# Tridiagonalisation in one program: the panel loop as a hardware loop, and written out

## The reference

```python
deg = jnp.sum(A, axis=0) + jnp.sum(A, axis=1) - jnp.diagonal(A)
L_norm = d_inv_sqrt[:, None] * (jnp.diag(deg) - A) * d_inv_sqrt[None, :]
_, U = jnp.linalg.eigh(L_norm)            # 1024 x 1024, symmetric
agg = jnp.einsum('mn,bnd->bmd', U.T, features)
...
return jnp.einsum('nm,bmd->bnd', U, out)
```

## Time and profile before

| | |
|---|---|
| median of 3 runs | 9222.39 us (9209.03 to 9224.98) |
| profiled execution: its own time | 9224.03 us |
| its span, first to last instruction | 9222.3 us |
| its mean granted clock of PE | 0.756 of full speed |
| first L401 to last L401 (panel 0 to panel 31) | 838.4 to 5724.6 us |
| busy over the span | PE 5701.9, DVE 6703.0, ACT 2708.2, POOL 1214.8 us |

### The profile page before, as it was taken

The page is one execution under the profiler, slowest core; times in us unless marked ns, Lnnn a source line. Parts: engine busy times, 40 slices in busy tenths (PEclk is TensorE's granted clock), DMA queues, the critical chain, the costliest instruction groups (busy, mean ns, idle before and its releaser), DMA issues. The chain is left out here.

```text
span 9222.3 us, 334698 instructions
## 1 busy us (share of the span) xinstructions
PE 5701.9 (62%) x138962; PEld 3872.5 (42%) x138962; DVE 6703.0 (73%) x32749; ACT 2708.2 (29%) x7811; POOL 1214.8 (13%) x5408
## 2 busy tenths in 40 slices
PE   5696778777788877777776554344434330036956
PEld 2364555555566666655665544101000000033446
DVE  3566666677677777777778888888888889954055
ACT  1442111111111111111113334566666650010046
POOL 0000111111122222222223333100000000000000
PEclk8898999999999999888665555555555555578989
DMA  1000000000000000000000000000000000000000
GB/s 38 1 1 20 4 4 4 4 4 4 4 4 4 4 4 4 4 4 4 4 4 4 4 4 4 1 0 0 0 0 0 0 0 0 0 0 1 0 19 19
DMA packets 24662, 42.83 MB, mean 5 GB/s; under 512 B 2464, under 2 KB 20128, under 8 KB 23200
## 3 DMA queue, kind: packets, MB, share of 16 engines
q1 hardware_dynamic: 23200, 21.70, 0.7%
HBM read 17.50 MB, written 4.19 MB: 2 GB/s over the span
## 5 line engine op out<-in xcount | busy, mean ns | idle before, releaser
L313 PE MATMUL tri_y<-L 128*32 128x256 f32 (+7 forms) x36792 | 1976.5, 345 | 11.8 <-issue 10.9
L313 PEld LDWEIGHTS tri_y<-L 128*32 128x32 f32 x36792 | 1195.6, 122 | 226.5 <-issue 50.6
L405 ACT ACTIVATE tri_mu<-tri_ring,tri_tiny 128x1 f32<-128x1 f32 x1022 | 267.1, 261 | 1985.4 <-PE tri_ring L296 1985.4
L1536 PE MATMUL ev_pairs<-ev_sgn,ident 128*128 128x448 bf16 x1024 | 428.8, 574 | 579.7 <-ACT ev_sgn L1501 579.7
L1660 DVE SCALAR_TENSOR_TENSOR ev_seq<-ev_seq,ev_rowG,ev_u 128x112 f32<-128x112 f32 x2048 | 682.8, 333 | 91.0 <-DVE ev_u L1645 2.3
L408 ACT ACTIVATE tri_sM<-tri_half_M,tri_s 128x8 f32<-128x8 f32 (+5 forms) x767 | 229.0, 299 | 1464.7 <-DVE tri_s L601 1464.7
L1645 DVE TENSOR_TENSOR ev_u<-ev_shifted,ev_seq 128x112 f32<-128x112 f32 x2048 | 560.4, 274 | 86.6 <-DVE ev_seq L1667 14.0
L1490 ACT ACTIVATE ev_shifted<-ev_x,ev_rowG 128x112 f32<-128x112 f32 x2112 | 613.0, 372 | 31.4 <-DVE ev_rowG L1617 31.4
L296 PE MATMUL tri_ring<-L 128*32 128x32 f32 (+25 forms) x35704 | 599.6, 206 | 3.3 <-issue 3.1
L296 PE MATMUL tri_k<-tri_kp,tri_half 128*32 128x1 f32 x6136 | 191.1, 184 | 615.3 <-DVE tri_x L609 614.8
L296 PEld LDWEIGHTS tri_ring<-L 128*32 128x32 f32 x35704 | 516.0, 118 | 3.7 <-issue 3.7
(11 more groups left out here) (660 smaller groups left out, 14148.8 us busy)
## 6 DMA issues: line engine op xcount, KB each, us to landing
adj<-in_adj_dram SPq DMA_DIRECT2D x12, 1024.0 KB, 8.1
x<-in_x_dram SPq DMA_DIRECT2D x8, 512.0 KB, 7.2
out_dram<-x SPq DMA_DIRECT2D x8, 512.0 KB, 6.6
gcn_w<-in_L_gnn_W_dram SPq DMA_DIRECT2D x2, 128.0 KB, 2.2
spec_w<-in_L_gnn_W_dram SPq DMA_DIRECT2D x2, 64.0 KB, 1.8
dot_wt<-in_L_gnn_W_dram SPq DMA_DIRECT2D x1, 64.0 KB, 1.8
dot_rows<-in_L_gnn_b_lin_dram SPq DMA_DIRECT2D x1, 64.0 KB, 2.7
dot_rows<-in_L_gnn_b_dram SPq DMA_DIRECT2D x1, 64.0 KB, 3.4
```

What stands on the lines that cost most here:

```text
L313: last = nc.tensor.matmul(y[32 * g:32 * g + 32, 0:T * 32], A[:, b + t, XC:XC + 1].broadcast_to([P, 32]), cols, start=(t == 0), stop=(t == ...
L405: nc.scalar.activation(mu[:, :], sigma, ACT.Sqrt, bias=tiny[:, :]).then_inc(root_ready, 1)
L1536: last = nc.tensor.matmul(sums[h], S["ident16"][:, :], sgn[:, h * (GRP // 2) + k:(h + 1) * (GRP // 2) + k, :].rearrange("p s w -> p (s w)" ...
```

## The change

The loop over a body's panels becomes a Python loop: each of the 32 panels is its own body, with a count of 1, so each has its own code on each of the four engines, and all counts are constants. The order of the work within a panel is what it was. One line fewer above shifts all later lines by one.

```diff
-        bodies = [(0, 0, 1, 1, NB_P), (0, 1, LP - 1, 0, NB_P)] + [(b, 0, LP, 0, NB_P) for b in range(1, NT - 1)] \
-            + [(NT - 1, 0, LP - 1, 0, NB_P), (NT - 1, LP - 1, 1, 0, NB_P - 1)]
+        bodies = [(b, p, 1, 1 if b == p == 0 else 0, NB_P - 1 if (b, p) == (NT - 1, LP - 1) else NB_P) for b in range(NT) for p in range(LP)]
...
             for k, (b, it0, cnt, s0, s1) in enumerate(bodies):
                 T = NT - b
-                with pe.Fori(0, cnt) as it:
+                for it in range(cnt):
                     pn = it + panels_before[k]
```

More of the change, by code:

```diff
@@ L257, in _ @@
                 T = NT - b
-                with pool.Fori(0, cnt) as it:
+                for it in range(cnt):
                     pool.wait_ge(window_ready, it + (panels_before[k] + 1))
@@ L390, in _ @@
                 T = NT - b
-                with act.Fori(0, cnt) as it:
+                for it in range(cnt):
                     pn = it + panels_before[k]
@@ L456, in _ @@
                 act_t = slice(b, NT)
-                with dve.Fori(0, cnt) as it:
+                for it in range(cnt):
                     pn = it + panels_before[k]
```

## The result

| | before | after |
|---|---|---|
| median of the runs | 9215.71 us (4 runs, 9206.53 to 9224.98) | 9134.27 us (4 runs, 9132.60 to 9150.17) |
| profiled execution | 9224.03 us | 9133.02 us |
| span | 9222.3 us | 9131.3 us |
| first to last start of L401 (L400 after) | 4886.3 us | 4789.1 us |

The changed kernel takes 0.9915 of the time before, 95% interval 0.9898 to 0.9933. Between the two profiled executions it is 91.0 us; the stage of the panels alone gives 97 us of it, and the rest of the program was 6 us longer in this execution. That rest is the same code in every kernel here, and it took 4336 to 4347 us in the twelve profiles (4336.0 and 4345.1 in the two of the kernel before), so it moves by some 10 us by itself.

The account below looks back on a forecast made before the run. A chain of short steps across engines bounds the panels, with late fetches after jumps back. 47.7 + 5.7 - 1.7 = 51.7 us off the profiled 9224.0 us gives 9172.3, median 9171 us; range 9154 to 9196 us.

Parts of the forecast that it names:

- What bounds the kernel, and what a jump is: Panels are a chain of short steps with no engine full; a jump back makes the instruction fetch start late.
- PE's branch of 3.3 to 4.5 us as the price: At panel ends, a jump back costs PE some 3.3 to 4.5 us; falling through takes 76 ns.
- The 22 jumps back go: 47.7 us: At panel entries, later panels become like the first of their width, gaining 47.7 us over 20 jumps.
- T = 8: 0: Jumped-to T = 8 panels were 3.7 us shorter, put down to the clock and counted as 0.
- ACT's registers: 5.7 us: Between last update and L397, constants replace ACT's window registers: 30 entries at 0.19 us, 5.7 us gained.
- DVE's wait on its own, 1.7 us lost: In 19 tails, the wait ahead of DVE's copy becomes its own instruction: 1.7 us lost, bounds 0 to 3.6.
- The code grows, at nothing: ACT and POOL fetch every panel's code, 22 panels more; costed at nothing.
- Rival A: At panel starts the stall stays, only the instructions themselves are saved: 9216 us; 6 in 100.
- Rival B: Straight code starves as ACT and POOL fetch 60 blocks: 86 us slower, 9308 us; 4 in 100.
- Rival C: In T=5 and T=4 the clock takes back 23.2 us (9194), or T=5 gains 12.7 us (9158); 10 in 100 each side.

Follow-up runs that it names:

- experiment 4: ACT's and POOL's loops alone written out, against the kernel before, PE and DVE keeping loops: 9210.26 us, ratio 0.9994.
- experiment 1: Kernel before with loops kept, plus a hint on PE and DVE that the jump back comes: 9171.96 us, ratio 0.9954.
- pe_flat: PE's loop alone written out, against the kernel before: 9197.56 us, ratio 0.9980.
- experiments 10 and 6: 10: changed kernel plus idle PE products at entry and in tail, 9102.80 us, ratio 0.9868; 6: changed kernel once more, 9139.67 us, ratio 0.9904.

## Why the prediction was wrong

- *What bounds the kernel, and what a jump is.* Right. The entries of panels jumped to were late for want of instructions: the packets start 0.98 to 1.28 us after DVE's branch does, hints alone took 45 us off the entries, and straight code 53 and 64.
- *PE's branch of 3.3 to 4.5 us as the price.* Right as a row, misleading as a price. DVE was late at the same entries, by 0.9 to 3.6 us more than where no jump had come: PE alone gained 20.9 us, DVE alone 26.6, both together 76.5.
- *The 22 jumps back go: 47.7 us.* This is the step that failed: "I take the first panel of a width as what every panel of that width becomes". It held for T = 3 and 1 (6.2 and 4.8 us gained over the width, against 6.2 and 4.2 and up to 0.9 each for the windows), and in its sum, though not panel by panel, nearly for T = 5 (15.2 against 12.7). T = 2 gave 10.1 against 6.9, T = 6 9.7 against 3.5, 9.1 of it in entries. In T = 7 it gave 3.6 us and 24.5 came (11.8 in the second profile), in T = 4 10.5 and 24.4 (23.8 in the second). The first panels of these widths ran in part at the lower clock themselves: without a jump, panel 4 had an entry at 0.71 and four slow steps, and panel 16 an entry at 0.50, so they were no picture of what the others could become. In T = 6 the first panel hid most of the excess in the same way, by a tail of 12.68 us at 0.73 where the other three had 10.01 (panel 9 at 1.00). That the four panels of T = 7 began slow was visible in the granted clock of the earlier trace rows, 0.96 and 0.95 against 0.98 in T = 8, and I took it as given.
- *T = 8: 0.* 2.3 and 4.6 us came, against 3.8 between the two profiles of before: nothing that shows.
- *ACT's registers: 5.7 us.* Right: 5.9 in every kernel in which ACT is written out, 0.5 or less in the others.
- *DVE's wait on its own, 1.7 us lost.* Right in size where the clock does not cover it: the tails of T = 8 grew by 0.28 us over the three panels that had registers before, 0.09 each. The changed kernel has 31 semaphore instructions at L471 that the kernel before lacks, 21 ns each, and those at L645 take 49 to 50 ns in place of 21. The register instructions (ALU_OP, FUSED_REGOPS) of PE and DVE took 32 to 65 ns each before.
- *The code grows, at nothing.* Right: experiment 4, 57 packets more, no wait. Whether the blocks of ACT and POOL came ahead of need or within the time in which both wait for others was not separated.
- *Rival A* falls with the branch rows and with experiment 1; its 0.1 us a jump is in no run, where PE's branch takes 76 ns falling through and 3.3 us or more at a jump. *Rival B* falls with experiment 4. *Rival C*, whose two widths are T = 5 and T = 4 at 0.91 to 0.94 and 0.83 to 0.85 granted, came nearest and was under-priced. I had let the clock go the good way in T = 5 alone, 12.7 us. It went the good way in T = 7 and T = 4, and the steps, 38 us in the first profile and 24 in the second, were no term of the sum: they, and 5 to 17 us more in the entries than their 47.7, are what the range lacked. How much of the steps belongs to the change is open: 14 of the 38 went again in the second profile, and the two profiles of before differ by 5.
- *The slower steps of before.* What lowers the clock for them stays open. The six profiles with both engines written out gained 24 to 39 us in steps, the five others with one of the two or both in a loop 5 to 17 against the first of before, so some of the gain goes with the change. But not one cause explains both widths. In T = 7 the sum over four panels varies by 12.7 us between executions of one program, fell in two kernels in which DVE or both engines were late at the entries (`pe_flat`, `act_pool_flat`), and with PE held was that of the second profile of the changed kernel. In T = 4 holding PE gave back 8 of 12.6 us, yet the kernel with hints, whose entries there are as early as the changed kernel's to 0.35 us on average, gained only 0.5 us in steps and tails. Whether the place of a panel in time, the length of the wait or the work before it decides was not separated.

## What to carry to other kernels

Where a hardware loop's body is long (2137 built instructions a panel on PE and 862 on DVE here, against 163 on ACT, whose jump took 50 ns at most), compare the first pass with the later ones, width by width, and read the branch by source line: one instruction that took 76 ns in one pass and 3.6 us in the next was waiting for a fetch here, and the packets of the instruction queues show it, by a start 0.93 to 1.20 us after the branch's, at 19 of 22. Look for it on every engine: here two were late at the same place and each hid the other's cost, and writing out one of them brought about a third of the gain. And where the granted clock moves between its levels around the stall (0.50 and 1.00 here), do not take a pass without the stall as a bound for the gain, since it too may be running slow, as panel 4's entry did at 0.71; bound the clock's part by the difference of a step at either level times the slow steps in *all* passes (here 1.65 us times 14 in T = 7), and take a second profile of each kernel before calling that part a gain.

## What was not expected of the hardware

- DVE's jump cost nothing in the branch itself (49 to 78 ns), and the packet of q14 started 0.98 to 1.28 us after it. The norm behind it starts 1.3 to 3.9 us after L401, and 0.24 to 0.43 us after it where no jump came; in T = 5 alone a second stall of 2.1 us follows between two neighbouring instructions, with a second packet of q14 in it at all three entries; in T = 4 the second packet starts ahead of the norm, and at the other jumps one alone starts before the norm's sum is read.
- A hint ahead of the branch cut PE's median from 3571 to 414 ns, but DVE then stood still inside steps, once for 2.8 us.
- One program's T = 7 panels took 747.7 us in one execution and 760.4 in another, at granted clocks of 0.97 to 0.98 and 0.96; its whole time varied by 12 and 18 us in two sets of four runs.
- Idle products of PE in its waits gained some 33 us more than the change alone (0.0036, the difference of the ratios of experiments 10 and 6, of 9223 us), though nothing was taken away.
